# Decoder layer on one core: the last batch's units set out anew over three banks, and the first k read back head by head

## The reference, cut to what matters

```python
# x (4, 512, 512), ctx (4, 512, 256), 16 heads of 32
def attn(x):                       # rope on q and k, causal
    q, k, v = rope(x @ Wq + bq), rope(x @ Wk + bk), x @ Wv + bv
    return softmax(mask(q @ k.T / sqrt(32))) @ v @ Wo + bo      # per head
def xattn(x, ctx):
    energy = (ctx @ Wq2.T + bq2) @ (ctx @ Wk2.T + bk2).T
    return x @ softmax(energy).T
def ffn(x):
    return (silu(x @ w_gate.T) * (x @ w_up.T)) @ w_down.T       # 2048 hidden
x = layernorm(x + attn(x))
x = layernorm(x + xattn(x, ctx))
x = layernorm(x + ffn(x))
```

## Time and profile before

| | |
|---|---|
| Median of 3 runs | 1050.85 us (1048.11 to 1050.95) |
| The profiled execution | 1048.29 us, of which 1046.5 us span |
| Mean granted TensorE clock | 0.978 |
| Busy: PE, DVE, ACT, POOL | 94%, 60%, 47%, 34% of the span |
| Chain that ended last: PE, ACT, DVE, issue | 79%, 6%, 5%, 5% |

### The profile page before, as it was taken

How to read it: one execution, slowest core, us unless ns; L and a number is a source line. 1 busy time by engine, 2 the same in 40 slices (tenths; PEclk the granted TensorE clock), 3 DMA queues, 4 the chain that set the end, 5 groups by cost and what they waited for, 6 DMA issues and landing times.

```text
span 1046.5 us, 15709 instructions
## 1 busy us (share of the span) xinstructions
PE 981.5 (94%) x5416; PEld 794.5 (76%) x5416; DVE 630.3 (60%) x1344; ACT 493.5 (47%) x1075; POOL 352.3 (34%) x353
## 2 busy tenths in 40 slices
PE   7688999999999868899999999999999999999995
PEld 5556777777777656688888788888788888788884
DVE  5577788878778766545544475544565444653343
ACT  5476767777767654344432334432334432333330
POOL 2566646655756521213111132012132112131112
PEclk9899999999999979899999999999999999999998
DMA  6966676855868730262222143222252221242301
GB/s 219 255 152 168 171 183 158 229 142 145 242 158 191 186 120 1 91 230 91 73 79 91 61 175 148 91 73 80 78 207 98 91 91 61 91 171 92 111 9 41
DMA packets 44862, 134.53 MB, mean 129 GB/s; under 512 B 5232, under 2 KB 5360, under 8 KB 41968
## 3 DMA queue, kind: packets, MB, share of 16 engines
q1 hardware_dynamic: 44784, 133.52, 42.1%
HBM read 104.14 MB, written 25.17 MB: 124 GB/s over the span
## 4 chain that ended last, share of the span: by engine, by line
PE 79%; ACT 6%; DVE 5%; issue 5%; POOL 2%; DMA 2%; SPq 1%; POOLq 0%; DVEq 0%; ACTq 0%
PE pu L523 17%; PE pg L523 17%; PE pd L523 16%; PE pj L478 11%; PE pj L523 5%; PE pv L514 4%; PE ps L489 3%; PE pa L502 2%; ACT prob L678 2%; PE pb L502 2%; DVE prob L874 2%; PE pj L529 1%; ACT pT L685 1%; PE pj L476 1%; DMA ks<-qk_scratch 1%
## 5 line engine op out<-in xcount | busy, mean ns | idle before, releaser
L1191 POOL TENSOR_TENSOR g_lo<-gated,g_hi 128x512 fp32r<-128x512 f32 x64 | 82.5, 1289 | 439.8 <-ACT g_hi L769 439.8
L678 ACT ACTIVATE prob<-prob,nmax 128x512 f32<-128x512 f32 (+3 forms) x256 | 143.7, 562 | 114.4 <-DVE nmax L874 114.2
L874 DVE CUSTOM_DVE_ANT_0 prob<-ps,mask 128x512 f32<-128x512 f32 (+3 forms) x256 | 122.8, 484 | 79.8 <-PE ps L489 76.0
L980 DVE TENSOR_TENSOR dn_lo<-f_raw,dn_hi 128x512 fp32r<-128x512 f32 x64 | 51.2, 801 | 121.2 <-ACT dn_hi L753 121.2
L489 PE MATMUL ps<-ks,qs 128*128 128x256 f32 (+2 forms) x256 | 107.0, 420 | 13.5 <-DMA ks<-qk_scratch 8.0
L1001 DVE SCALAR_TENSOR_TENSOR half<-th,pg 128x512 f32<-128x512 f32 x64 | 43.9, 687 | 104.4 <-ACT th L760 104.4
L523 PE MATMUL pd<-dn_hi,g_hi 128*128 128x512 f32 x256 | 101.2, 395 | 0.2 <-POOL g_lo L1191 0.2
L760 ACT ACTIVATE th<-pg 128x512 f32<-128x512 f32 x64 | 38.3, 598 | 131.6 <-PE pg L523 131.6
L523 PE MATMUL pd<-dn_lo,g_hi 128*128 128x512 f32 x256 | 99.8, 390 | 0.0
L523 PE MATMUL pd<-dn_hi,g_lo 128*128 128x512 f32 x256 | 99.6, 389 | 0.0
L769 ACT CAST g_hi<-gated 128x512 fp32r<-128x512 f32 x64 | 39.7, 620 | 120.4 <-DVE gated L1008 120.4
(11 more groups left out here) (162 smaller groups left out, 2226.4 us busy)
## 6 DMA issues: line engine op xcount, KB each, us to landing
f_raw<-in_w_ffn SPq DMA_DIRECT2D x64, 768.0 KB, 4.3
qs<-qk_scratch SPq DMA_DIRECT2D x64, 256.0 KB, 4.8
ks<-qk_scratch SPq DMA_DIRECT2D x64, 256.0 KB, 7.8
qk_scratch<-qk_hi SPq DMA_DIRECT2D x32, 256.0 KB, 2.0
qk_scratch<-raw SPq DMA_DIRECT2D x32, 256.0 KB, 2.1
res<-in_x SPq DMA_DIRECT2D x4, 1024.0 KB, 4.9
x_scratch<-res SPq DMA_DIRECT2D x4, 1024.0 KB, 5.8
x<-x_scratch SPq DMA_DIRECT2D x4, 1024.0 KB, 4.8
```

What stands on the lines that cost most here:

```text
L678: act.activation(prob[:, t % PROBS, 0:w], prob[:, t % PROBS, 0:w], ACT.Exp, bias=nmax[:, n % 2, i:i + 1], scale=-1.0, accum_out=rsum[:, n ...
L874: dve.tensor_tensor_reduce(prob[:, t % PROBS, 0:w], ps[:, t % 2, 0:w], mask[:, S - w:S], -D ** -0.5, 3e38, ALU.add, ALU.min, accum_out=nma ...
L980: dve.tensor_tensor(dn_lo[:, i % 2, :], f_raw[i % NR][:, 2 * KT * P:], dn_hi[:, i % 2, :].bitcast(F32), ALU.subtract).then_inc(dnlo_done, 1)
L1191: pool.tensor_tensor(g_lo[:, i % 2, :], gated[:], g_hi[:, i % 2, :].bitcast(F32), ALU.subtract).then_inc(glo_done, 1)
```

## The change

The units from `q14` on are taken out of the rule and written by hand in a list `LAST` that names the bank of each. A third bank is used, `over[2]`, which is `pv` between two `weighted`. Each bank has its own semaphore of filled units, and a unit waits only for the one before it on its bank. Units on bank 2 wait for the `normalize` before them, and `weighted` waits until they are moved out.

- `q15` moves from slot 211 to 203 (beside `o8`), `k15` from 216 to 208 (beside `o9`), the context's `c` from 223 and 224 to 206 and 209, the four `e` from 229 to 234 to 214 to 222, the four `t` from 227 to 235 to 223 to 230, the four `a` from 236 to 239 to 234 to 238, `u1` from 255 to 253. `o10` and `o11` take three slots of four matmuls each.
- `SPLIT_CONTEXT` goes from 208 to 202 on ACT and to 203 on POOL. `x` is loaded for it at 211 instead of 219.
- The exponential of an `e` comes two slots after it, the low parts of `t`, `a`, `u` two (DVE), and DVE's first FFN cut at 260 instead of 257. `r15` stays at 261.
- Tiles are laid out otherwise in SBUF; `cqk` shares its place with `c_raw`, so SP's load of a later context waits until the context part before it has been cut (`cqklo_done`), and no longer for `clo_done`.
- `first_stack` reads the first group back: q in four DMAs as before, on a semaphore of its own; k in sixteen of 64 KB, head by head, with a semaphore for each head. The score waits for its own head only. `SPLIT_LATE` moves by up to three slots.

```diff
-SPLIT_LATE = {(3, 0): 5, ("o", 0): 7, ("o", 1): 11, ("o", 2): 14, ("o", 3): 16}
+SPLIT_LATE = {(3, 0): 8, ("o", 0): 10, ("o", 1): 12, ("o", 2): 14, ("o", 3): 17}
-LOAD_CONTEXT, SPLIT_CONTEXT, LOAD_X1, LOAD_F = 196, 208, 219, 241
+LOAD_CONTEXT, SPLIT_CONTEXT, LOAD_X1, LOAD_F = 196, 202, 211, 241
-CONTEXT = [(("c", 0), 223, (6,)), (("c", 1), 224, (6,)),
-           (("t", 0), 227, (4,)), (("t", 1), 228, (4,)), (("e", 0), 229, (3,)), (("e", 1), 230, (3,)),
-           (("e", 2), 232, (3,)), (("t", 2), 233, (4,)), (("e", 3), 234, (3,)), (("t", 3), 235, (4,)),
-           (("a", 0), 236, (4,)), (("a", 1), 237, (4,)), (("a", 2), 238, (4,)), (("a", 3), 239, (4,)),
-           (("m", 0), 241, (4, 4, 4)), (("m", 1), 243, (4, 4, 4)), (("m", 2), 246, (4, 4, 4)), (("m", 3), 250, (4, 4, 4)),
-           (("u", 0), 252, (4,)), (("u", 1), 255, (4,)), (("u", 2), 256, (4,)), (("u", 3), 257, (4,))]
+LAST = [(("q", 14), 195, (3, 3, 3, 3), 0), (("r", 11), 199, (4,), 1), (("k", 14), 200, (4, 4, 4), 0),
+        (("q", 15), 203, (3, 3, 3, 3), 1), (("o", 8), 203, (3, 3, 3, 3), 2), (("c", 0), 206, (6,), 0),
+        (("k", 15), 208, (4, 4, 4), 1), (("o", 9), 208, (4, 4, 4), 2), (("c", 1), 209, (6,), 0),
+        (("e", 0), 214, (3,), 0), (("r", 12), 215, (4,), 1), (("e", 1), 218, (3,), 1), (("e", 2), 219, (3,), 0),
+        (("o", 10), 219, (4, 4, 4), 2), (("e", 3), 222, (3,), 1), (("o", 11), 223, (4, 4, 4), 2),
+        (("t", 0), 223, (4,), 0), (("t", 1), 226, (4,), 1), (("t", 2), 227, (4,), 0), (("t", 3), 230, (4,), 1),
+        (("r", 13), 231, (4,), 0), (("a", 0), 234, (4,), 1), (("a", 1), 235, (4,), 0), (("a", 2), 237, (4,), 2),
+        (("a", 3), 238, (4,), 1), (("m", 0), 242, (4, 4, 4), 0), (("m", 1), 243, (4, 4, 4), 1), (("r", 14), 247, (4,), 0),
+        (("m", 2), 248, (4, 4, 4), 1), (("m", 3), 250, (4, 4, 4), 0), (("u", 0), 252, (4,), 2), (("u", 1), 253, (4,), 1),
+        (("u", 2), 255, (4,), 0), (("u", 3), 257, (4,), 1), (("r", 15), 261, (4,), 0),
+        (("o", 12), 267, (12,), 1), (("o", 13), 268, (12,), 0), (("o", 14), 269, (12,), 1), (("o", 15), 270, (12,), 0)]
...
-PLACE = {key: n for n, (key, start, counts) in enumerate(UNITS)}
+BANKS = [[unit[0] for unit in UNITS if unit[3] == n] for n in range(3)]
+PLACE = {unit[0]: (unit[3], BANKS[unit[3]].index(unit[0])) for unit in UNITS}
...
+    over = [pj[:, 0, :], pj[:, 1, :], pv[:]]
...
+        def first_stack():
+            for u in range(2):
+                sp.wait_ge(stored[u], 32)
+                for r in range(1 if u == 0 else 4):
+                    for j in range(4):
+                        rows = (2 * (j // 2 if u == 0 else j % 2) + u) * P
+                        if u == 0:
+                            sp.dma_start(qs0[D * j:D * j + D, :, :].bitcast(F32),
+                                         scratch[rows:rows + P, :].rearrange("(r d) s -> d r s", d=D)).then_inc(first_q, 16)
+                        else:
+                            sp.dma_start(ks0[D * j:D * j + D, r, :].bitcast(F32),
+                                         scratch[rows + D * r:rows + D * r + D, :]).then_inc(first_k[r], 16)
...
-                if i == 0 and PLACE[key] >= 2:
-                    emptied(pe, UNITS[PLACE[key] - 2][0])
+                if i == 0 and index:
+                    emptied(pe, BANKS[at][index - 1])
+                if i == 0 and at == 2:
+                    pe.wait_ge(o_done, (STARTS[key] - AV) // TILES + 1)
...
+            if n == 0 and t % ST == 0:
+                if t == 0:
+                    pe.wait_ge(first_q, 64)
+                pe.wait_ge(first_k[r], 64)
...
+            for key in BANKS[2]:
+                if 0 < TILES * n + AV - STARTS[key] < TILES:
+                    emptied(pe, key)
...
-            if t == FIRST_GU:
+            if t == FIRST_GU + 3:
                 gu_half(0)
...
-            if t == SPLIT_CONTEXT:
+            if t == SPLIT_CONTEXT + 1:
                 context_rest(0)
```

More of the change, by code:

```diff
@@ L76, in units @@
 def units():
-    out = list(CONTEXT)
+    out = []
     for n in range(GROUPS):
@@ L196, in program @@
     xhi_done, xlo_done = sem("xhi_done"), sem("xlo_done")
-    pj_full = sem("pj_full")
+    pj_full = [sem(f"pj_full{n}") for n in range(3)]
     raw_done = [sem(f"raw_done{u}") for u in range(2)]
@@ L202, in program @@
     stacked = [sem(f"stacked{u}") for u in range(2)]
+    first_q, first_k = sem("first_q"), [sem(f"first_k{r}") for r in range(4)]
     v_done = sem("v_done")
@@ L612, in _ @@
                 scores(t)
-            for key, start, counts in UNITS:
+            for key, start, counts, _ in UNITS:
                 if start <= t < start + len(counts):
@@ L656, in project @@
             kind, n = key
-            src = pj[:, PLACE[key] % 2, :]
+            src = over[PLACE[key][0]]
             full(act, key)
@@ L709, in context_move @@
             filled(act, b, cqk_full, "c", u)
-            act.activation(cqk[:, u, :], pj[:, bank(b, "c", u), :], ACT.Identity, bias=pbias[:, u:u + 1]).then_inc(cqk_moved, 1)
+            act.activation(cqk[:, u, :], over[bank(b, "c", u)], ACT.Identity, bias=pbias[:, u:u + 1]).then_inc(cqk_moved, 1)
         def context_cast(b, u):
@@ L717, in energy_exp @@
             act.wait_ge(nemax_done, KT * b + n + 1)
-            act.activation(e[:, n, :], pj[:, bank(b, "e", n), :], ACT.Exp, bias=nemax[:, n:n + 1], scale=1.0,
+            act.activation(e[:, n, :], over[bank(b, "e", n)], ACT.Exp, bias=nemax[:, n:n + 1], scale=1.0,
                            accum_out=esum[:, n:n + 1]).then_inc(e_done, 1)
@@ L724, in t_half @@
             filled(act, b, later, kind, n)
-            act.copy(hi[:, :, n * P:(n + 1) * P], pj[:, bank(b, kind, n), :].rearrange("p (k m) -> p k m", m=P)).then_inc(done, 1)
+            act.copy(hi[:, :, n * P:(n + 1) * P], over[bank(b, kind, n)].rearrange("p (k m) -> p k m", m=P)).then_inc(done, 1)
         def beside(b, kind, n):
@@ L896, in add_bias @@
             dve.wait_ge(late_in, 48)
[L897 removed]
+            dve.tensor_tensor(bo[:], over[PLACE["b", 0][0]], bo[:], ALU.add).then_inc(bo_done, 1)
         def recips(n):
@@ L915, in summed @@
             full(dve, ("o", n))
-            dve.tensor_tensor(res[:, n % ST, :], pj[:, PLACE["o", n] % 2, :], res[:, n % ST, :], ALU.add).then_inc(z_done, 1)
+            dve.tensor_tensor(res[:, n % ST, :], over[PLACE["o", n][0]], res[:, n % ST, :], ALU.add).then_inc(z_done, 1)
         def moments(n):
@@ L947, in mixed @@
             filled(dve, b, m_full, "m", n)
-            dve.tensor_tensor(x[:, n, :], pj[:, bank(b, "m", n), :], x[:, n, :], ALU.add).then_inc(z2_done[0], 1)
+            dve.tensor_tensor(x[:, n, :], over[bank(b, "m", n)], x[:, n, :], ALU.add).then_inc(z2_done[0], 1)
         def finished(b, s):
```

75 lines of the change are left out of this document (40 added, 35 removed).

## The result

| | before | changed |
|---|---|---|
| median of 4 runs, us | 1050.46 (1048.11 to 1050.95) | 1038.69 (1038.01 to 1040.66) |
| ratio to before | | 0.9889, 95% 0.9867 to 0.9911 |
| the profiled execution, us | 1048.29 | 1038.01 |
| its span, us | 1046.5 | 1036.2 |
| its mean granted clock | 0.978 | 0.990 |

The kernel became faster by 1.1%, some 12 us; the forecast was 1036.5, in a range of 1027 to 1046. The clock line of the page, the answer to the earlier trace rows, has lost the dips of slices 2 and 15 (the start, and the context's units); the one of slice 17, at the end of the attention, is left.

The account below looks back on a forecast made before the run. PE, busy nearly all the time, was taken to bound the kernel outside three places. -2.3 + 11.9 - 16.8 - 1.7 - 3.8 = -12.7 from 1048.29 gave 1035.6, plus 1 for the base: 1036.5 us, range 1027 to 1046.

Parts of the forecast that it names:

- Start: Up to slot 203: k read head by head starts the first score 4.1 us earlier; 2.3 us gained, bounds 0 and 4.1.
- Rival 3: First k load: each 64 KB DMA takes as long as 256 KB (1.3 us), start loses 7, 1045.5 us; chance 0.08.
- the estimate beside it: First k load: at 0.95 us per 64 KB, sixteen DMAs end at 48.2 us and the start gains about nothing.
- ACT, then the scores, wait for that add: Start: POOL's unbroken run from 48.2 us to k2's add, near 59.1, holds the scores; 1.8 us gained, not 4.1.
- Slots 203 to 223: Dense slots taking more matmuls, with a 4.4 us wait before `c0`: 11.9 us longer, 43.7 for 31.8.
- e0: Slots 203 to 223: POOL's backlog reaches this unit through the low parts of the context's query and key; 1 us.
- small waits: Slots 212 to 223: DVE, with `e` work beside `o10`, is the fullest engine; 2 us added.
- Slots 224 to 243: Light slots whose waits between context units go: 16.8 us gained, 27.0 for 43.8, bounds 24.5 and 33.
- rival 5: Slots 224 to 254: thin work drops PE's clock to 1.2 GHz, PE becomes the bound, kernel possibly slower; chance 0.10.
- Rival 4: Context part gives nothing, another wait holds the light slots; only start and tail pay, 1042 to 1047 us; chance 0.12.
- rival 2: Slots 203 to 223: the wait before `c0` is covered and DVE keeps up, 1027 us (1025 to 1031); chance 0.18.
- The tail: Behind the last score: DVE's cuts move back and 1.9 us of `u2`, `u3` bank waits go; 3.8 gained, bounds 2 and 6.

Follow-up runs that it names:

- the last batch: Changed kernel with the old first load of k and old `SPLIT_LATE`, so only the new order from `q14` on: 1043.36 us, ratio 0.9928 to the kernel before.

## Why the prediction was right

**Start.** *Right:* a small DMA doesn't take as long as a large one. Head 0 was complete at 33.2 and the last head at 36.3 us. At the end it was the issues that set the pace and not the bytes, since the time to landing fell from 5.1 us for the first of the sixteen to 2.1 for the last. Rival 3 falls with it: these landed 0.27 us apart. So does the estimate beside it, which laid sixteen times the 0.95 us for 64 KB end to end that the Trainium skill's page "DMA: Bandwidth & Descriptors", section "Bandwidth", states. The page measured that for DMAs over 128 partitions issued from GpSimd, and these went from SyncE to 32 partitions each. The runs here speak against the end to end and not against the page's row. As for the first score, q had landed at 32.1, not 33.0, hence 33.3 and not 34.3.

*Half right:* the step "ACT, then the scores, wait for that add". The add is in the chain, and the run before it began at 48.30 us for my 48.2. The 48.2 was luck: I had it from slot 8 at the old pace, but what set it was ACT's wait for the store of q1, without which the run began at 44.66. The price was there too (2.2 us of 5.1 lost until slot 20, where I had 1.8 of 4.1), but with that wait gone it was gone as well. The prediction counted the issues moved past `res` and did not ask what else was queued behind them on SP, the store that frees `raw`, nor that ACT would come to that store earlier. The term is also too small in the medians, 4.7 to 5.5 us for 2.3. I priced the standing alone; the half clock is a part of the rest (1.5 to 2.3 us in the two profiles of the old start, 0 to 1.7 in the new), and the remainder is not located.

**Slots 203 to 223.** The place, the releaser and the size of the stand (3.83 for 4.4) and the low clock behind it (3.4 us for 5) were right, and so was `e0` (1.07 for 1.0). The term came out 1.4 us too low. For small waits I had 2 us, put down to DVE's load; they took 3.5: `o9` 0.5, the `weighted` of group 12 1.17, `o11` 0.83 (all three for DVE's `res`), `e1` 1.04 (for ACT's move of r12). The first three, 2.5 us, are the price of the third bank itself, on which a unit or a `weighted` waits until the unit before it is moved out. The prediction had no such price. Less the shorter stand and low clock that explains half of the 1.4; the rest is not located.

**Slots 224 to 243.** 26.5 us for 27.0, at a clock of 1.00 and with no wait of 1 us. PE idled for 17% of them (21.98 of 26.60 us busy), in short gaps, and the clock stayed full: rival 5 falls. Rival 4 falls too, since the context's slots gave even a little more than forecast, and rival 2 for the wait at `c0` was there.

**Slots 244 to 254.** 18.7 us for 18.2; the clock was back at 1.00 (0.91 in the earlier trace rows), as predicted.

**The tail** is the term that was mis-sized: 2.2 us for 3.8, and 7.30 us from the last score to the last `weighted`, where I had said under 6. DVE in the changed kernel from 412 us to the end of the attention:

```profile
412.32 1.28 DVE L980 TENSOR_TENSOR x2T_lo<-pj,x2T_hi 128x512 fp32r<-128x512 f32 x2
413.93 0.69 DVE L918 COPY pT<-pb 128x512 f32<-128x512 f32 x1 [0.33 <-PE pb L535]
414.54 0.41 DVE L923 COPY pT<-pc 128x256 f32<-128x256 f32 x1
414.87 0.68 DVE L980 TENSOR_TENSOR x2T_lo<-pj,x2T_hi 128x512 fp32r<-128x512 f32 x1
...
416.09 1.22 DVE L1010 TENSOR_TENSOR gu_lo<-f_raw,gu_hi 128x1024 fp32r<-128x1024 f32 x1
```

The low part of `u3` and `gu_lo` did move behind the move of `pT`, unlike the earlier trace rows. But the waits of `u2` and `u3` were not on top of that: from the last score to the end of that move DVE is idle for 0.33 us, so it is DVE's own work that fills the stretch, and waits of PE beside a full DVE could not be given back a second time. Before, DVE had only some 1.1 us of idle between the last score and the last `weighted` to lose. I added the two as if they lay end to end.

**Why the total came out right all the same.** By luck. In the medians the last batch gave 7.5 us where its four terms had 10.4, and the start 2.4 to 3.2 more than its 2.3: the two errors nearly cancel, -11.8 for -12.7. The ratios behind these figures have intervals of plus or minus 1.3 to 2.4 us. The rest of the 2.2 us between forecast and median is the base: the profiled execution before lay 2.2 us under the median of its runs, and I had put back 1.

## What to carry to other kernels

Where a DMA is cut into many, follow the issuing queue past them to the first store that frees a buffer: the wait for it is the price, when the engine that needs the buffer comes sooner than before, and a load that isn't urgent can go behind it. Where work is pulled forward, move its casts on the slower engines by as much, for a stand in a dense stretch costs its own length and the low clock behind it. Waits of one engine count as a gain only up to the idle time of the engine that runs beside them.

## What the runs showed of the hardware

- The sixteen DMAs of 64 KB were issued 0.46 us apart and landed 0.27 us apart: 15 of them in the 4.1 us from the first landing to the last, the time in which three of 256 KB had landed behind the first before. The first took 5.1 us to land, behind q's bytes, and the last 2.1.
- The store of 256 KB that was issued behind two loads landed 8.4 us after its issue, at 44.3 us; with those loads behind it, it landed 2.7 us after its issue, at 37.4 us.
- TensorE stood 3.0 us before the first score, and the granted clock behind it was at 2.4 GHz throughout in one execution and at 1.2 GHz for 3.4 us in another. With a stand of 8.0 us it fell inside the stand and was at 1.2 GHz for 6.8 us in one and 10.2 us in the other. What follows a stand differed between executions though the stand did not. That spread is as large as the terms argued about here.
- In slots 224 to 243 of the changed kernel TensorE was busy for 21.98 of 26.60 us, with no wait of 1 us, and the granted clock stayed at 2.4 GHz.
